# Per-head norms of the first attention layer: one power on GpSimd for a bit-pattern guess with Newton steps

## The chip, the cores and the metric

The kernel runs on one core of a Trainium2 chip. The metric is the device time of one execution in microseconds (us). The kernel before took 2115.83 us in the median of 3 runs, from 2112.31 to 2118.05. The trace comes from one further, profiled execution.

## The reference, cut to what matters

The input is 16 batches of 512 tokens with 128 features. Two transformer layers run over it, each with an attention and a mixture of experts, each behind a layer norm and with a residual. The change concerns the attention of the first layer. It has 16 heads of 8 features; q and k are scaled to length one for each head, and no softmax is taken:

```
def _l2norm(t):
    n = jnp.sqrt(jnp.sum(t * t, axis=-1, keepdims=True))
    return t / jnp.maximum(n, 1e-12)
q = _l2norm(proj(Wq, bq)); k = _l2norm(proj(Wk, bk)); v = proj(Wv, bv)
sim = jnp.einsum('bhid,bhjd->bhij', q, k)
out = jnp.einsum('bhij,bhjd->bhid', sim / n ** sigmoid(m), v)
```

The kernel forms k^T v before it multiplies by q, so only the two scalings stand between the projection and the next products: for each token 32 numbers, 1/sqrt(max(sum of squares, 1e-24)), one for each head of q and of k.

## The kernel before, in words

A batch of 512 tokens is held as 128 partitions by Q = 4 rows of 128 features. Batches run through a software pipeline: `looped` (L276 is its loop) alternates an `x_phase` and a `y_phase`, and in one turn four batches are worked on at once under the names f (front: first attention and first experts), r (the second layer's projections), b (the second layer's scores, softmax and outputs) and t (tail: output projection, residual, router). Three turns are written out ahead of the loop, 13 run in it, and some phases follow it. After the loop comes the second layer's expert routing and the experts, which the change doesn't touch.

Each engine has its own program and its order is written by hand; engines wait for each other by semaphores alone. In the `y_phase` the vector engine (DVE) runs, in this order: `r_norm`, `f_bias`, `r_center`, `f_bias`, `f_l2`, `r_rest` 0, `f_scale`, `r_rest` 1, `outputs` 0 (the copy of the product in `bo` to `oT`, L1379), `norm` 0 (L1386, L1388), `f_kvm`, and so on to the gates of the first experts and `norm` 3, with which the turn of the loop ends.

- `f_l2` waits for the squares `sq` that the scalar engine (ACT, L1026) makes of q and k, sums them by head (L1180), takes the maximum with 1e-24 (L1181), makes a first guess of 1/sqrt by integer arithmetic on the bits (L1182) and does one Newton step (L1187 to L1189). `f_scale` does two more and multiplies k and q by the result `rn` (L1196). All of these but L1196 are done in two halves of two rows each: while a half waits for its own result, the other runs. Each half is followed by a wait of DVE on its own semaphore.
- `r_rest` (L1372) subtracts the rounded part of the second layer's q or k from the product in `facc`. GpSimd (POOL) then rounds the rest and subtracts again (L485, L487). SP writes the three parts of both to memory (`part_dmas`) and, when both are written, reads them back spread over partitions as QT and KT (`back_dmas`, L329).
- `power` (L451) is POOL's 1/sqrt: a TENSOR_TENSOR with the operation pow and a tile of -0.5, `mhalf`, 128 columns wide. It is used for the layer norms' four numbers a partition.
- PE (TensorE), in the same phase, runs the second layer's scores of a pair of heads (`pair_scores`, 10 products with their masks, L579 and L581), and between them `outputs` (L838), `turn_outputs` (L845, which waits for DVE's `oT`) and the front batch's products: `f_kvq` (L620), `f_kv` (L627, L630), which waits for L1196, `f_kvo`, `f_out`. Scores go through three banks of PSUM, which ACT's exponentials (L1017) empty.

Of the kernel before, what the change touches and what calls it, by code (L numbers as in the profile page):

```python
# [14 lines left out]
F32, BF16, F16, I32, I16 = mybir.dt.float32, mybir.dt.bfloat16, mybir.dt.float16, mybir.dt.int32, mybir.dt.int16  # L15
ALU = mybir.AluOpType
# [3 lines left out]
P = 128  # L20
BATCH, SEQ, D = 16, 512, 128
Q = SEQ // P
TOK = BATCH * SEQ
TILES = TOK // P
HEADS, HD = 16, 8
# [7 lines left out]
L2_EPS_SQ = 1e-24  # L33
# [11 lines left out]
def build_kernel(nc, a, out):  # L45
    ctx = ExitStack()
    with ctx:
# [5 lines left out]
        def sb1(name, shape, dt=F32):  # L53

            return early.enter_context(nc.sbuf_tensor(name, shape, dt))

        def sem(name):
            return ctx.enter_context(nc.semaphore(name))
# [55 lines left out]
        f_rs = sb1("f_rs", [P, Q])  # L114
        n2 = sb1("n2", [P, Q, 2 * HEADS])
        rn = sb1("rn", [P, Q, 2 * HEADS])
        rt = sb1("rt", [P, Q, 2 * HEADS])
        f_n = sb1("f_n", [P, Q, D])
        f_nT = sb1("f_nT", [P, SEQ])
        kvq = sb1("kvq", [P, Q, 3 * D])  # L120
# [64 lines left out]
        def sb3(name, shape, dt=F32):  # L185
# [51 lines left out]
        contrib = [sb(f"contrib{i}", [P, CC, D]) for i in range(2)]  # L237


        names = """s_wfront s_wexperts s_wback s_cst s_one s_scal s_x s_lnf s_xres s_varf s_rsf s_T1 s_nT1 s_kvq s_kvqe s_sq  # L240
            s_kqn s_kvt s_kvm s_qT s_qnT s_kvo s_kvoc s_at0 s_x1 s_x1n s_T2 s_nT2 s_lgm s_lge s_exf s_lgx s_gp s_gTp s_gT
            s_h1 s_h3 s_gb s_gbc s_sil s_t s_h s_hs s_ym s_yT s_yTt s_x2 s_fc
            s_pad s_lnb s_varb s_rsb s_T3 s_nT3 s_q s_k s_v s_p1 s_r1 s_p2 s_p3 s_vp s_qkw s_qk0 s_qk1 s_S s_red s_nmp s_nmt
# [4 lines left out]
        S = {n: sem(n) for n in names}  # L248
# [3 lines left out]
        def apart(eng):  # L252

            eng.nop(nofuse=True)
# [165 lines left out]
        def _(pool):  # L420
# [28 lines left out]
            def power(dst, src, ready, done, count):  # L449
                pool.wait_ge(S[ready], count)  # L450
                pool.tensor_tensor(dst, src, mhalf[:, 0:src.shape[-1]], ALU.pow).then_inc(S[done], 1)  # L451
# [25 lines left out]
            def y_phase(b, f, r, t):  # L477
                if r is not None:
                    power(b_rs[:], b_ve[:], "s_varb", "s_rsb", r + 1)
                if r is not None:  # L480
                    for w in range(2):

                        pool.wait_ge(S["s_r1"], 2 * r + w + 1)
                        apart(pool)
                        pool.tensor_copy(qkp[:, w, 1], qkr[:, w]).then_inc(S["s_p2"], 1)  # L485
                        pool.wait_ge(S["s_p2"], 2 * r + w + 1)
                        pool.tensor_tensor(qkp[:, w, 2], qkr[:, w], qkp[:, w, 1], ALU.subtract).then_inc(S["s_p3"], 1)  # L487
                if f is not None:
                    power(f_rs[:, 0:Q], f_ve[:, 0:Q], "s_varf", "s_rsf", 2 * f + 2)

            looped(pool, x_phase, y_phase)
            for m in range(1 - GJ, GJ):

# [598 lines left out]
        def _(dve):  # L1092
# [35 lines left out]
                    dve.wait_ge(self.sem, self.b * self.per + self.n)  # L1128
                    apart(dve)

            fc, mc, rc, tc = Steps("s_fc", 67), Steps("s_mstep", 6), Steps("s_rstep", 8), Steps("s_tc", 8)

            def stats(step, x, st, mv):

# [41 lines left out]
            def f_l2(f):  # L1176


                dve.wait_ge(S["s_sq"], f + 1)
                fc.halves(lambda q: dve.tensor_reduce(n2[:, q], sq[:, q].rearrange("p q (g d) -> p (q g) d", d=HD), X, ALU.add))  # L1180
                fc.halves(lambda q: dve.tensor_scalar(n2[:, q], n2[:, q], L2_EPS_SQ, None, ALU.max))  # L1181
                fc.halves(lambda q: dve.tensor_scalar(rn[:, q].bitcast(I32), n2[:, q].bitcast(I32), -0.5, float(0x5F3759DF), ALU.mult, ALU.add))  # L1182
                f_newton(1)

            def f_newton(steps):
                for _ in range(steps):
                    fc.halves(lambda q: dve.scalar_tensor_tensor(rt[:, q], n2[:, q], -0.5, rn[:, q], ALU.mult, ALU.mult))  # L1187
                    fc.halves(lambda q: dve.tensor_tensor(rt[:, q], rt[:, q], rn[:, q], ALU.mult))
                    fc.halves(lambda q: dve.scalar_tensor_tensor(rn[:, q], rt[:, q], 1.5, rn[:, q], ALU.add, ALU.mult))  # L1189

            def f_scale(f):
                f_newton(2)
                fc.join()
                for w in range(2):
                    heads = kvq[:, :, 2 * w * D:(2 * w + 1) * D].rearrange("p q (h d) -> p q h d", d=HD)
                    last = dve.tensor_tensor(heads, heads, rn[:, :, w * HEADS:(w + 1) * HEADS, None].to_broadcast([P, Q, HEADS, HD]), ALU.mult)  # L1196
                last.then_inc(S["s_kqn"], 1)
# [176 lines left out]
            def y_phase(b, f, r, t):  # L1374
# [26 lines left out]
                if_r(r_center)  # L1401
                if_f(lambda f: f_bias(f, 1))
                if_f(f_l2)
                if_r(r_rest, 0)
                if_f(f_scale)
                if_r(r_rest, 1)
                outputs(0)
# [227 lines left out]
```

## Time and profile before

| | before |
|---|---|
| median of 3 runs | 2115.83 us |
| the profiled execution | 2124.21 us |
| its span, first to last instruction | 2122.4 us |
| granted TensorE clock, mean | 0.881 of full |
| busy: PE, DVE, ACT, POOL | 1623.8, 1243.4, 793.3, 502.1 us |
| one turn of the loop, about | 106 us |

Busy time is the sum of the instructions of an engine; waits and register instructions aren't in it. The chain of waits starts at the last instruction and goes back from each step to what released it, so what stands on it sets the time. "issue" in a view is time in which an engine waited for nothing that the profile shows.

### The profile page before, as it was taken

How to read it: one execution, taken by the hardware profiler on the slowest of the kernel's cores; microseconds unless marked ns; L12 is line 12 of the kernel's file. 1: busy time of each engine (PE TensorE's matmuls, PEld its weight loads, DVE VectorE, ACT ScalarE, POOL GpSimd, SP SyncE). 2: the span in 40 equal slices, each digit the busy share in tenths (PEclk: the TensorE clock that was granted, in tenths of full speed). 3: DMA queues.
4: the chain of work that ended last, by engine and by line, in shares of the span. 5: the costliest groups of instructions: out<-in, count | busy, mean ns of one | idle time of the engine just before them, and what ended most of it. 6: DMA issues, size and time to landing. Idle time of an engine off the chain costs nothing.

```text
span 2122.4 us, 34602 instructions
## 1 busy us (share of the span) xinstructions
PE 1623.8 (77%) x10136; PEld 908.2 (43%) x10136; DVE 1243.4 (59%) x3733; ACT 793.3 (37%) x1515; POOL 502.1 (24%) x487
## 2 busy tenths in 40 slices
PE   3779888888888888888888888888899781137675
PEld 2345444444444444444444444444454441135554
DVE  5466757575757575757575757575766436861111
ACT  1225252525252525252525252525253342233331
POOL 2321212121212121212121212121212002007887
PEclk7879999989898989899999898999999875568888
DMA  2032231313131313131313031313031400023443
GB/s 64 19 46 41 31 53 24 52 24 58 18 56 20 58 18 58 18 54 22 56 19 59 17 59 17 56 20 59 17 56 21 65 7 10 0 35 84 90 92 59
DMA packets 113451, 86.62 MB, mean 41 GB/s; under 512 B 21440, under 2 KB 107840, under 8 KB 113344
## 3 DMA queue, kind: packets, MB, share of 16 engines
q1 hardware_dynamic: 102080, 76.64, 21.7%
q0 software_dynamic: 11264, 8.92, 3.0%
q14 instruction: 85, 0.70, 0.2%
q8 instruction: 22, 0.36, 0.1%
HBM read 59.02 MB, written 25.72 MB: 40 GB/s over the span
## 4 chain that ended last, share of the span: by engine, by line
PE 44%; issue 18%; DVE 17%; ACT 5%; POOL 5%; DMA 5%; SPq 2%; DVEq 1%; ACTq 0%; POOLq 0%
PE ba L579 6%; PE fa L668 5%; PE facc L694 5%; PE ba L584 4%; PE fa L684 4%; PE bo L838 4%; POOL out L551 3%; ACT probs L1017 2%; SPq L329 2%; DVE passed L1464 2%; PE ba L581 2%; PE ba L586 2%; DVE nm L1264 2%; DMA KT<-qk_parts 1%; POOL got L521 1%
## 5 line engine op out<-in xcount | busy, mean ns | idle before, releaser
L584 PE MATMUL ba<-KT,QT 72*128 72x512 bf16 (+3 forms) x1024 | 263.9, 321 | 188.5 <-DVE nm L1264 130.5
L1017 ACT ACTIVATE probs<-ba 128x512 f32<-128x512 f32 x640 | 330.3, 634 | 94.9 <-PE ba L581 94.0
L458 POOL TENSOR_TENSOR hh<-th,gb 128x512 f32<-128x512 f32 x128 | 162.1, 1267 | 713.5 <-ACT gb L970 437.2
L1264 DVE TENSOR_REDUCE nm<-ba 128x1 f32<-128x512 f32 x256 | 174.8, 683 | 191.7 <-issue 142.6
L579 PE MATMUL ba<-QT,KT 75*128 75x512 bf16 (+3 forms) x1024 | 254.8, 311 | 35.3 <-ACT probs L1017 28.9
L584 PEld LDWEIGHTS ba<-KT,QT 72*128 72x128 bf16 x1024 | 105.2, 103 | 350.2 <-DVE nm L1264 155.2
L586 PE MATMUL ba<-mask_q,identb 128*128 128x128 bf16 x1024 | 201.7, 231 | 0.0
L581 PE MATMUL ba<-mask_k,identb 128*128 128x128 bf16 x1024 | 197.1, 225 | 0.0
L668 PE MATMUL fa<-f_nT,w 128*128 128x512 f32 x320 | 187.1, 669 | 2.3 <-ACT sc L1048 1.2
L684 PE MATMUL fa<-f_nT,w 128*128 128x512 f32 x320 | 181.0, 649 | 0.0
L986 ACT ACTIVATE sil<-fa 128x512 f32<-128x512 f32 x160 | 95.1, 594 | 213.8 <-PE fa L668 213.6
L970 ACT ACTIVATE gb<-fa 128x512 f32<-128x512 f32 x128 | 76.3, 596 | 260.8 <-PE fa L676 260.7
L579 PEld LDWEIGHTS ba<-QT,KT 75*128 75x128 bf16 x1024 | 102.4, 100 | 155.2 <-ACT probs L1017 100.8
L694 PE MATMUL facc<-hh,w 128*128 128x512 f32 x320 | 166.2, 602 | 0.0
L838 PE MATMUL bo<-probs,vp 128*32 128x512 f32 (+3 forms) x2048 | 155.6, 445 | 0.8 <-DVE ao L1388 0.8
L1266 DVE TENSOR_REDUCE nm<-ba 128x1 f32<-128x384 f32 x256 | 140.6, 549 | 24.5 <-PE ba L586 24.4
L586 PEld LDWEIGHTS ba<-mask_q,identb 128*128 128x128 bf16 x1024 | 106.5, 104 | 82.6 <-issue 80.3
L451 POOL TENSOR_TENSOR b_rs<-b_ve,mhalf 128x4 f32<-128x4 f32 x48 | 48.5, 1010 | 338.8 <-DVE b_ve L1364 228.1
L1379 DVE COPY oT<-bo 128x512 f32<-128x512 f32 x64 | 44.1, 689 | 116.7 <-PE bo L838 116.7
L551 POOL DMA_INDIRECT out<-contrib,cur x64 | 100.7, 1573 | 29.4 <-issue 18.6
L838 PEld LDWEIGHTS bo<-probs,vp 128*32 128x32 f32 x2048 | 60.9, 112 | 101.6 <-issue 76.2
L581 PEld LDWEIGHTS ba<-mask_k,identb 128*128 128x128 bf16 x1024 | 103.3, 101 | 1.8 <-issue 0.9
(283 smaller groups left out, 2681.2 us busy)
## 6 DMA issues: line engine op xcount, KB each, us to landing
QT<-qk_parts SPq DMA_DIRECT2D x288, 64.0 KB
KT<-qk_parts SPq DMA_DIRECT2D x288, 64.0 KB
qk_parts<-qkp SPq DMA_DIRECT2D x32, 384.0 KB, 2.5
fc<-in_L_ffn_fc_weight SPq DMA_DIRECT2D x32, 256.0 KB, 2.9
xin<-in_L_attn_x SPq DMA_DIRECT2D x16, 256.0 KB, 14.3
out<-x SPq DMA_DIRECT2D x16, 256.0 KB, 2.3
xn_rows<-row SPq DMA_DIRECT2D x16, 256.0 KB, 2.4
w<-in_L_w SPq DMA_DIRECT2D x3, 640.0 KB, 6.9
```

What stands on the lines that cost most here:

```text
L458: pool.tensor_tensor(hh[:, e % 2], th[:, e % 2], gb[:, e % 2], ALU.mult).then_inc(S["s_h"], 1)
L551: pool.indirect_dma_start(out_rows, bass.IndirectOffsetOnAxis(cur[k][:, c:c + 1], 0), contrib[k % 2][:, c], None, compute_op=ALU.add).then ...
L579: pe.matmul(bank[:, col:col + w], lhsT=KT[0:K_ROWS, head, blk * P:(blk + 1) * P], rhs=QT[0:K_ROWS, head, blk * P:], start=True, stop=False)
L581: last = pe.matmul(bank[:, col:col + P], lhsT=identb[:], rhs=mask_k[:], start=False, stop=True)
L584: pe.matmul(bank[:, col:col + w], lhsT=QT[0:QK_ROWS, head, blk * P:(blk + 1) * P], rhs=KT[0:QK_ROWS, head, 0:w], start=True, stop=False)
L586: last = pe.matmul(bank[:, col + w - P:col + w], lhsT=identb[:], rhs=mask_q[:], start=False, stop=True)
L668: pe.matmul(fa[0][:], lhsT=w1[:, e], rhs=f_nT[:], start=True, stop=True).then_inc(S["s_h1"], 1)
L684: pe.matmul(fa[1][:], lhsT=w3[:, e], rhs=f_nT[:], start=True, stop=True).then_inc(S["s_h3"], 1)
L694: pe.matmul(facc[:], lhsT=w2[:, e], rhs=hh[:, e % 2], start=e == 0, stop=e == U0 - 1).then_inc(S["s_ym"], 1)
L838: last = pe.matmul(bo[32 * j:32 * j + 32, blk * P:], lhsT=vp[:, blk, 4 * k + j], rhs=prob_block(4 * k + j, blk), start=blk == 0, stop=blk ...
L1017: act.activation(probs[:, pair % 3, f_], ba[n % 3][:], ACT.Exp, scale=SCALE).then_inc(S["s_exp"], 1)
L1264: last = dve.tensor_reduce(nm[:, 3, h:h + 1], bank[:], X, ALU.max, negate=True)
```

## The change

The guess, the three Newton steps and the tile `rt` go. DVE takes the maximum in one instruction over all 128 numbers and signals `s_n2`; POOL raises them to -0.5 in one instruction and signals `s_rn`; `f_scale` on DVE waits for that. On POOL the power stands in the `y_phase` behind the power of the second layer's norm and ahead of the two casts and subtractions of the rests. On DVE `r_rest` 0 stays between `f_l2` and `f_scale`.

```
@@ y_phase of POOL @@
                 if r is not None:
                     power(b_rs[:], b_ve[:], "s_varb", "s_rsb", r + 1)
+                if f is not None:
+                    power(rn[:].rearrange("p q g -> p (q g)"), n2[:].rearrange("p q g -> p (q g)"), "s_n2", "s_rn", f + 1)
                 if r is not None:
                     for w in range(2):
@@ DVE @@
-            fc, mc, rc, tc = Steps("s_fc", 67), Steps("s_mstep", 6), Steps("s_rstep", 8), Steps("s_tc", 8)
+            fc, mc, rc, tc = Steps("s_fc", 45), Steps("s_mstep", 6), Steps("s_rstep", 8), Steps("s_tc", 8)
...
                 fc.halves(lambda q: dve.tensor_reduce(n2[:, q], sq[:, q].rearrange("p q (g d) -> p q g d", d=HD), X, ALU.add))
-                fc.halves(lambda q: dve.tensor_scalar(n2[:, q], n2[:, q], L2_EPS_SQ, None, ALU.max))
-                fc.halves(lambda q: dve.tensor_scalar(rn[:, q].bitcast(I32), n2[:, q].bitcast(I32), -0.5, float(0x5F3759DF), ALU.mult, ALU.add))
-                f_newton(1)
-
-            def f_newton(steps):
-                for _ in range(steps):
-                    fc.halves(lambda q: dve.scalar_tensor_tensor(rt[:, q], n2[:, q], -0.5, rn[:, q], ALU.mult, ALU.mult))
-                    fc.halves(lambda q: dve.tensor_tensor(rt[:, q], rt[:, q], rn[:, q], ALU.mult))
-                    fc.halves(lambda q: dve.scalar_tensor_tensor(rn[:, q], rt[:, q], 1.5, rn[:, q], ALU.add, ALU.mult))
-
+                fc.join()
+                dve.tensor_scalar(n2[:], n2[:], L2_EPS_SQ, None, ALU.max).then_inc(S["s_n2"], 1)
             def f_scale(f):
-                f_newton(2)
-                fc.join()
+                dve.wait_ge(S["s_rn"], f + 1)
                 for w in range(2):
```

## Rows read from the trace of the kernel before

**Rows 1.** The page: the span and each engine's busy time, share and instructions.

```profile
span 2122.4 us, 34602 instructions
PE 1623.8 (77%) x10136; PEld 908.2 (43%) x10136; DVE 1243.4 (59%) x3733; ACT 793.3 (37%) x1515; POOL 502.1 (24%) x487
```

**Rows 2.** The chain of waits, 1015 to 1058 us: start us, us, what.

```profile
1017.82 1.11 ACT sq L1026
...
1023.75 0.82 issue
...
1026.58 0.69 DVE kvq L1196
1027.26 0.60 DVE qkr L1372
1027.86 0.61 DVE oT L1379
1028.52 0.66 PE bo L845 x4
```

**Rows 3.** Timeline of DVE: start us, us, line, tile; idle before and releaser.

```profile
1014.11 0.17 DVE L1364 TENSOR_SCALAR b_ve<-b_mv 128x4 f32<-128x4 f32 x1 [0.47 <-DVE b_mv L1138]
...
1015.40 1.12 DVE L1143 TENSOR_SCALAR b_n<-x,b_mv,b_rs 128x128 f32 x4
...
1018.95 1.28 DVE L1180 TENSOR_REDUCE n<-sq 128x64 f32<-128x512 f32 x2 [1.50 <-ACT sq L1026]
...
1021.90 0.68 DVE L1372 TENSOR_TENSOR qkr<-facc,qkp 128x512 f32<-128x512 f32 x1
1022.50 0.35 DVE L1187 SCALAR_TENSOR_TENSOR rt<-n,rn 128x64 f32<-128x64 f32 x2
1022.82 0.72 DVE L1188 TENSOR_TENSOR rt<-rt,rn 128x64 f32<-128x64 f32 x2
1023.51 1.27 DVE L1189 SCALAR_TENSOR_TENSOR rn<-rt,rn 128x64 f32<-128x64 f32 x2
...
1025.11 0.40 DVE L1188 TENSOR_TENSOR rt<-rt,rn 128x64 f32<-128x64 f32 x2
1025.46 0.40 DVE L1189 SCALAR_TENSOR_TENSOR rn<-rt,rn 128x64 f32<-128x64 f32 x2
1025.97 1.29 DVE L1196 TENSOR_TENSOR kvq<-kvq,rn 128x512 f32<-128x512 f32 x2
...
1027.78 0.68 DVE L1379 COPY oT<-bo 128x512 f32<-128x512 f32 x1
...
1030.84 0.29 DVE L1201 TENSOR_TENSOR kvm<-fa,kv_scale 128x128 f32<-128x128 f32 x1 [1.04 <-PE fa L627]
```

**Rows 4.** Timeline of PE in the same turn.

```profile
1024.24 2.36 PE L838 MATMUL bo<-probs,vp 128*32 128x512 f32 x32
```

**Rows 5.** Waits (us in total, times, longest), and DVE's and PE's timeline at the jump.

```profile
DVE nm L1264 <- issue: 142.6, 12, 12.9
1068.25 0.69 DVE L1264 TENSOR_REDUCE nm<-ba 128x1 f32<-128x512 f32 x1 [12.40 <-issue]
1069.00 0.50 PE L584 MATMUL ba<-KT,QT 72*128 72x384 bf16 x1 [11.40 <-DVE nm L1264]
```

**Rows 6.** Timeline of POOL in the turn of rows 3.

```profile
1014.36 1.01 POOL L451 TENSOR_TENSOR b_rs<-b_ve,mhalf 128x4 f32<-128x4 f32 x1 [14.77 <-DVE b_ve L1364]
1022.72 0.61 POOL L485 CAST qkp<-qkr 128x512 bf16<-128x512 f32 x1 [7.35 <-DVE qkr L1372]
1023.41 1.16 POOL L487 TENSOR_TENSOR qkp<-qkr,qkp 128x512 bf16<-128x512 f32 x1
```

**Rows 7.** Timeline of DVE in the first batch.

```profile
26.94 1.28 DVE L1180 TENSOR_REDUCE n<-sq 128x64 f32<-128x512 f32 x2 [1.12 <-ACT sq L1026]
...
32.22 1.29 DVE L1196 TENSOR_TENSOR kvq<-kvq,rn 128x512 f32<-128x512 f32 x2
```

**Rows 8.** Groups of POOL by line and shape: count, busy us, mean ns, idle before.

```profile
L458 POOL TENSOR_TENSOR hh<-th,gb 128x512 f32<-128x512 f32 x128 | 162.1, 1267 | 713.5 <-ACT gb L970 437.2 <-DVE th L1253 269.9 <-PE facc L694 6.4
L451 POOL TENSOR_TENSOR b_rs<-b_ve,mhalf 128x4 f32<-128x4 f32 x48 | 48.5, 1010 | 338.8 <-DVE b_ve L1364 228.1 <-DVE b_ve L1286 100.4 <-DVE b_ve L1296 10.3
L451 POOL TENSOR_TENSOR f_rs<-f_ve,mhalf 128x4 f32<-128x4 f32 x32 | 32.3, 1010 | 203.3 <-DVE f_ve L1210 191.5 <-DVE f_ve L1165 11.7
L516 POOL TENSOR_TENSOR ahead<-weight 128x8 f32<-128x8 f32 x1 | 0.2, 205 | 0.0
```

**Rows 9.** Stretches: busy us (count) by engine, granted clock, DMA share, GB/s.

```profile
1065.00:1069.00 4.00, 0.00 (x1) 0.01 (x1) 0.75 (x2) 0.00 (x0) 0.00 (x0) 0.50 0.59 67
1069.00:1071.00 2.00, 2.00 (x6) 1.04 (x7) 2.00 (x5) 0.00 (x0) 0.00 (x0) 0.50 0.59 66
1071.00:1073.00 2.00, 2.00 (x9) 0.90 (x7) 0.72 (x3) 0.90 (x2) 0.08 (x1) 0.52 0.29 58
1073.00:1075.00 2.00, 2.00 (x12) 1.10 (x11) 1.38 (x3) 0.78 (x2) 1.18 (x1) 1.00 0.00 0
```

**Rows 10.** DMA queues, 1055 to 1069 us: packets, MB, share of 16 engines.

```profile
q1 hardware_dynamic: 1247, 1.03, 61.7%
q14 instruction: 2, 0.02, 0.9%
```

**Rows 11.** One turn as a stretch, columns as in rows 9.

```profile
1008.00:1113.00 105.00, 86.67 (x569) 46.17 (x568) 68.01 (x209) 42.70 (x84) 19.89 (x18) 0.95 0.26 38
```

More of the change, by code:

```diff
@@ L116, in build_kernel @@
         rn = sb1("rn", [P, Q, 2 * HEADS])
-        rt = sb1("rt", [P, Q, 2 * HEADS])
         f_n = sb1("f_n", [P, Q, D])
@@ L237, in build_kernel @@
         contrib = [sb(f"contrib{i}", [P, CC, D]) for i in range(2)]
-        names = """s_wfront s_wexperts s_wback s_cst s_one s_scal s_x s_lnf s_xres s_varf s_rsf s_T1 s_nT1 s_kvq s_kvqe s_sq
+        names = """s_wfront s_wexperts s_wback s_cst s_one s_scal s_x s_lnf s_xres s_varf s_rsf s_T1 s_nT1 s_kvq s_kvqe s_sq s_n2 s_rn
             s_kqn s_kvt s_kvm s_qT s_qnT s_kvo s_kvoc s_at0 s_x1 s_x1n s_T2 s_nT2 s_lgm s_lge s_exf s_lgx s_gp s_gTp s_gT
```

## The prediction

> **What bounds the kernel now.** I read the page first. No engine fills the span: PE is busy 77% of it, DVE 59%, POOL 24% [rows 1]. So the question is which chain sets the pace of a batch, and what the share of an engine is worth has to be read in the stage that changes. The chain of waits came next. In the stage that holds the change (1017 to 1030 us, one of the steady turns of the loop) it runs ACT `sq`, then DVE through the Newton steps to `kvq` L1196, `qkr` L1372 and the copy `oT` L1379, and only then PE's transposes L845 [rows 2]. The reader is to see that DVE, not PE, is on the path there: PE had finished the product that `oT` copies at 1024.24 + 2.36 = 1026.60, and `oT` started at 1027.78 [rows 3, 4]. Everything in `f_scale` therefore stands in front of the batch, and an engine that makes `f_scale` late makes the batch late by as much. The same turn ends with 12.4 us in which DVE and PE stand still after the jump back of the loop [rows 5]; I come to it below.
>
> **What is removed.** 22 DVE instructions a batch (11 steps in two halves): the two maxima, the two guesses, 18 halves of Newton steps. In time that is the stretch from the end of the sum of squares, 1018.95 + 1.28 = 1020.23, to the start of L1196 at 1025.97: 5.74 us [rows 3]. It is not all arithmetic: 0.60 us of it is the rest L1372 (1021.90 to 1022.50), which stays, and about 1.2 us is lost while POOL casts and subtracts (1022.72 to 1024.57) [rows 6]: the two halves of L1188 took 0.72 instead of 0.40 and those of L1189 1.27 instead of 0.40 [rows 3]. For the very first batch, with no other work beside it, the stretch is 26.94 + 1.28 = 28.22 to 32.22, so 4.0 us [rows 7].
>
> **What is added.** One maximum over 128x128 on DVE, at most the 0.29 us of L1201, another one of that size [rows 3]; a semaphore from DVE to POOL (0.08 us: L1364 ends at 1014.28, L451 starts at 1014.36) and one back (0.03 us: L451 ends at 1015.37, L1143 starts at 1015.40) [rows 3, 6]; and one power of 128 columns on POOL, of length P.
>
> P is not in the trace: all 80 powers there have 4 columns and take 1.01 us [rows 8]. Bounds from the nearest rows: an ordinary two-input POOL instruction takes 0.205 us for 8 columns and 1.267 us for 512 [rows 8], 2.1 ns a column. If the power's excess of 1.010 - 0.205 = 0.805 us is paid once an instruction, P = 1.01 + 124 x 0.0021 = 1.3 us. If it is paid by the column, that is 0.201 us a column, and P = 1.01 + 124 x 0.201 = 25.9 us. If all of the 1.01 us scales, P = 32 x 1.01 = 32.3 us. I take 25.9: L516 does everything that an instruction of this shape needs once, for twice the columns, in 0.205 us, so the excess belongs to evaluating the function, and that is done for each column; a once-only cost would be four times that whole instruction.
>
> A rule of the Trainium skill speaks for the short end. The GPSIMD Engine Reference (section 3.1) gives about 2.6 cycles an element for a two-input elementwise instruction at 1.2 GHz; an estimate from it is 0.27 us for 124 more columns and P = 1.28 us. The slope between L516 and L458 agrees with it, but the L451 rows do not fit it at all, since by it a power of 4 columns would cost about what L516 costs. By it the sum would be that of the first rival.
>
> **The sum.** With P = 25.9 the power ends at 1020.23 + 0.3 + 0.08 + 25.9 = 1046.5 and `f_scale` starts at 1046.6 instead of 1025.97: 20.6 us late. For the first batch it is 0.3 + 0.1 + 25.9 - 4.0 = 22.3. Nothing covers it. Queued on DVE behind the wait are L1196, the second rest, the copies of PE's output and all later steps of the phase; the first rest stands ahead of the wait and runs under the power. On POOL, behind the power, stand the cast and subtraction of the first rest; they would have run at 1022.72 and now start at 1046.5. They gate the write of the parts and so SP's loads of QT and KT, but SP waits for the second rest's parts too before it loads, and those come after L1196 in any case, so the loads shift with the batch and not beyond it. PE can still do the first output product and three scores of the next pair, as it does now, and then waits for `oT`.
>
> Two smaller terms. The cast and subtraction now meet L1196, which reads two SBUF tensors as L1188 and L1189 do: I add the 1.2 us they lost, for 15 batches, 18 us. And PE stands still for about 20 us in each phase. After the 11.4 us of idling at the loop's end the granted clock is 0.50 (1.2 GHz) in the rows, and it stays there for about 4 us of work before 1.00 (2.4 GHz) is back [rows 9]; 4 us at half speed cost 2 us, in the 14 phases that have scores: 28 us.
>
> Sum: 15 x 20.6 + 22.3 = 331, + 18 + 28 = **+377 us**. The profiled execution took 2124.2 us (span 2122.4), 0.4% above the median of the three runs, 2115.8, and its stages are taken as those of a median run: 2116 + 377 = **2493 us**.
>
> **The loop's jump.** DVE starts its first instruction of the next turn 12.4 us after the last one of this turn, 12 of these waits sum to 142.6 us and nothing in the program releases them [rows 5]. In that stretch queue 14, which carries instructions, moves 2 packets, while the loads of QT and KT fill the queues [rows 10]. The change takes 22 of DVE's 209 instructions of a turn [rows 11], and their waits, out of the loop. I price that at nothing: the jump is still there and still falls into the loads of QT and KT. The bounds are both sides of nothing: -143 us if the shorter body no longer has to be brought in again, and up to +60 (12 turns x 5 us, a little under half of a present wait) if the packets come at a worse moment.
>
> The Trainium skill (Runtime: NRT & Kernel Launch, section Instruction fetch mechanics) says that a taken branch whose target is no longer in the engine's instruction window stalls on a DMA fetch. The two packets in the stretch agree; whether the shorter loop would fit no run here shows.
>
> **Rivals.**
> 1. *The power's excess is paid once* (P = 1.3). It is the other side: `f_scale` is then ready at 1022.5, behind the first rest, meets POOL's cast and subtraction (+1.2), and `oT` starts when PE is done, at 1026.6 instead of 1027.78. 14 x 1.2 + 2 x 2.3 (first two batches: 4.0 - 1.7) = 21 us less: 2095 us. It decides from P = 1025.97 - 1020.23 - 0.3 - 0.1 = 5.3 us, 35 ns a column: below it the change gains, above it loses. For it: POOL's ordinary slope is 2.1 ns. Against: the 0.8 us that no other small POOL instruction has.
> 2. *Columns overlap inside the instruction*, so that further ones cost half of what the first four did: P = 13.5, 8.2 us a batch, 16 x 8.2 + 18 + 28 = +177: 2293 us. No row tells it from the forecast.
> 3. *The loop body, shorter, stays in place*, with the slow power: 2493 - 143 = 2350 us. For it: 22 of 209 instructions of a turn go [rows 11]. Against it: a tenth is little, and the trace shows no loop of DVE that is as long and does not wait.
>
> **How the numbers follow.** Forecast 0.70, rival 1 0.10, rival 2 0.13, rival 3 0.07. The forecast's own range goes from 2440 (without the clock and contention terms) to 2640 (P = 32.3 adds 16 x 6.4 = 102, the fetches up to 60; both in full are unlikely). The full range reaches down over rivals 3 and 2: **2200 to 2640**; what it leaves out is rival 1 and the tails, under 2 in 10. A difference under 0.3% (about 6 us) can't be told from none in this kernel. Faster: rival 1 less its part near the break-even, 0.09; within 0.3%: 0.02; slower: 0.89.
>
> **What would show it.** In the profile after: a POOL group `rn<-n,mhalf` 128x128 x16 near 26 us (right), near 1.3 or 13 us (rivals 1, 2); DVE idle before the scaling of `kvq` (L1196 now), released by POOL, some 24 us each, 16 times; DVE's busy time down by the Newton steps, worth nothing; a granted clock of 0.50 around the restart in mid-phase; the issue wait of the loop's jump still near 12 us (rival 3: gone). The prediction is wrong if the power is under 10 us, or if the batch grows by clearly less or more than the power outlasts the Newton steps.

## The result, and the profile after

| | before | after |
|---|---|---|
| median in the same runs | 2116.94 us (2112.31 to 2118.59, 4 runs) | 2429.31 us (2422.09 to 2435.56, 4 runs) |
| ratio over the runs, 95% interval | 1 | 1.1491, 1.1449 to 1.1533 |
| the profiled execution | 2124.21 us, span 2122.4 | 2434.28 us, span 2432.5 |
| granted TensorE clock, mean | 0.881 | 0.833 |

The change costs 312 us where +377 were forecast. First the page of the changed kernel, the lines that answer to [rows 1] and the shares of its chain of waits:

```profile
span 2432.5 us, 33657 instructions
PE 1660.3 (68%) x10136; PEld 937.9 (39%) x10136; DVE 1189.3 (49%) x3397; ACT 795.2 (33%) x1515; POOL 838.9 (34%) x503
PE 35%; issue 23%; POOL 19%; DVE 12%; DMA 3%; SPq 2%; ACT 2%; DVEq 1%; POOLq 0%; ACTq 0%
```

DVE's busy time fell by 54.1 us (1243.4 to 1189.3), and that bought nothing. POOL's rose by 337, and POOL, 5% of the chain before, is now 19% of it. Three groups of after and, as the last line, the scaling of before say where (busy us, mean ns of one, then the idle time ahead and its releaser):

```profile
L450 POOL TENSOR_TENSOR rn<-n,mhalf 128x128 f32<-128x128 f32 x16 | 332.5, 20781 | 94.5 <-DVE n L1183 94.5
L450 POOL TENSOR_TENSOR b_rs<-b_ve,mhalf 128x4 f32<-128x4 f32 x48 | 48.5, 1011 | 335.0 <-DVE b_ve L1356 223.0 <-DVE b_ve L1278 102.0 <-DVE b_ve L1288 10.0
L1188 DVE TENSOR_TENSOR kvq<-kvq,rn 128x512 f32<-128x512 f32 x32 | 40.8, 1314 | 305.4 <-POOL rn L450 305.4
L1196 DVE TENSOR_TENSOR kvq<-kvq,rn 128x512 f32<-128x512 f32 x32 | 20.7, 689 | 1.7
```

The new power takes 20.78 us each time, and DVE stands 305 us in front of the scaling of `kvq`, released by it. The scaling itself takes 1314 ns instead of 689: it now starts together with POOL's cast (1104.22 and 1104.14 below). Now one turn in time order, DVE, POOL and PE one after the other (start, duration, instruction, in brackets the idle time ahead and what ended it):

```profile
1081.72 1.28 DVE L1181 TENSOR_REDUCE n<-sq 128x64 f32<-128x512 f32 x2 [1.73 <-ACT sq L1027]
1083.10 0.23 DVE L1183 TENSOR_SCALAR n<-n 128x128 f32<-128x128 f32 x1
1084.66 0.69 DVE L1364 TENSOR_TENSOR qkr<-facc,qkp 128x512 f32<-128x512 f32 x1 [1.33 <-ACT qkp L971]
1104.22 2.63 DVE L1188 TENSOR_TENSOR kvq<-kvq,rn 128x512 f32<-128x512 f32 x2 [18.87 <-POOL rn L450]
1106.78 0.68 DVE L1364 TENSOR_TENSOR qkr<-facc,qkp 128x512 f32<-128x512 f32 x1
1107.38 0.67 DVE L1371 COPY oT<-bo 128x512 f32<-128x512 f32 x1
```

```profile
1083.41 20.78 POOL L450 TENSOR_TENSOR rn<-n,mhalf 128x128 f32<-128x128 f32 x1 [5.63 <-DVE n L1183]
1104.14 0.61 POOL L486 CAST qkp<-qkr 128x512 bf16<-128x512 f32 x1
1104.83 1.47 POOL L488 TENSOR_TENSOR qkp<-qkr,qkp 128x512 bf16<-128x512 f32 x1
```

```profile
1087.02 2.36 PE L839 MATMUL bo<-probs,vp 128*32 128x512 f32 x32
1108.11 1.12 PE L846 MATMUL bo<-ident,oT 128*128 128x128 f32 x4 [17.74 <-DVE oT L1371]
```

The chain is the one forecast: power, scaling, second rest, copy, transposes. PE finished the product that L1371 copies at 1087.02 + 2.36 = 1089.38, went on with scores until 1090.37 and was idle from there to 1108.11. From the windows of the same turn (length, then busy time of PE, PEld, DVE, ACT and POOL with counts, granted clock, DMA share, GB/s), the clock of that pause, which answers to [rows 9]:

```profile
1092.00:1094.00 2.00, 0.00 (x0) 0.00 (x0) 0.00 (x0) 0.00 (x0) 2.00 (x1) 1.00 0.00 0
1096.00:1098.00 2.00, 0.00 (x0) 0.00 (x0) 0.00 (x0) 0.00 (x0) 2.00 (x1) 0.50 0.00 0
1110.00:1112.00 2.00, 2.00 (x12) 1.94 (x11) 0.00 (x0) 1.10 (x2) 0.00 (x0) 0.50 0.57 197
1112.00:1114.00 2.00, 1.99 (x17) 1.43 (x17) 0.29 (x1) 1.30 (x3) 0.00 (x0) 1.00 0.15 42
```

PE works again from 1108.11 and gets 0.50 until 1112. The loop's jump waits as before [rows 5]; the first line is of the waits (total, times, longest), the second of DMA in the stretch 1137 to 1150:

```profile
DVE nm L1256 <- issue: 143.8, 12, 13.4
q14 instruction: 2, 0.02, 0.8%
```

To see where 310 us of span went, I cut each turn at DVE's own instructions (the jump runs from the branch to the first register instruction behind it) and took the mean over the turns with a jump ahead of them (12 of 13), in us:

| stage of a turn | before | after | e4_busy | e5_pages | e8_castfirst |
|---|---|---|---|---|---|
| wait at the jump | 11.97 | 12.08 | 12.45 | 0.29 | 11.92 |
| x_phase, to the residual sum L1355 | 49.50 | 49.81 | 49.60 | 51.27 | 49.86 |
| to the sum of squares L1180 | 7.45 | 7.45 | 7.45 | 7.45 | 7.45 |
| sum of squares to scaling L1196 | 7.02 | 22.50 | 22.50 | 22.51 | 26.39 |
| scaling to first `oT` L1379 | 1.98 | 3.16 | 3.16 | 3.16 | 1.81 |
| to second `oT` | 8.00 | 9.98 | 7.98 | 10.17 | 10.25 |
| to third `oT` | 7.87 | 7.87 | 7.87 | 7.87 | 7.87 |
| to fourth `oT` | 8.15 | 9.24 | 8.27 | 8.41 | 9.48 |
| to the branch | 3.85 | 4.16 | 4.16 | 3.81 | 4.16 |
| one turn | 105.80 | 126.25 | 123.46 | 114.93 | 129.19 |

After against before: +20.45 in each of 12 turns (245.5), +16.4 in the loop's first turn, +50.6 in the three batches ahead of it, -2.4 behind the loop: 310.1, the difference of the spans.

### The profile page after: what moved, and what is told of

Same layout as the page of the kernel before. It is cut to its first block, busy times and chain, and to the rows that moved or that the text cites. A ratio compares the mean times of both kernels' runs of the same rounds, so it can differ in the third digit from the quotient of the medians.

```text
span 2432.5 us, 33657 instructions
## 1 busy us (share of the span) xinstructions
PE 1660.3 (68%) x10136; PEld 937.9 (39%) x10136; DVE 1189.3 (49%) x3397; ACT 795.2 (33%) x1515; POOL 838.9 (34%) x503
## 4 chain that ended last, share of the span: by engine, by line
PE 35%; issue 23%; POOL 19%; DVE 12%; DMA 3%; SPq 2%; ACT 2%; DVEq 1%; POOLq 0%; ACTq 0%
POOL rn L450 13%; PE ba L580 5%; PE bo L839 5%; PE fa L669 4%; PE fa L685 3%; PE ba L585 3%; POOL out L552 3%; PE facc L695 3%; PE ba L582 2%; DVE passed L1456 2%; SPq L328 2%; POOL got L522 1%; PE ba L587 1%; PE bo L846 1%; DMA xin<-in_L_attn_x 1%
## 5 line engine op out<-in xcount | busy, mean ns | idle before, releaser
L450 POOL TENSOR_TENSOR rn<-n,mhalf 128x128 f32<-128x128 f32 x16 | 332.5, 20781 | 94.5 <-DVE n L1183 94.5
L580 PE MATMUL ba<-QT,KT 75*128 75x512 bf16 (+3 forms) x1024 | 264.9, 320 | 35.2 <-ACT probs L1018 28.7
L1256 DVE TENSOR_REDUCE nm<-ba 128x1 f32<-128x512 f32 x256 | 174.4, 681 | 191.4 <-issue 143.8
L846 PE MATMUL bo<-ident,oT 128*128 128x128 f32 x256 | 46.8, 313 | 252.6 <-DVE oT L1371 252.6
L582 PE MATMUL ba<-mask_k,identb 128*128 128x128 bf16 x1024 | 204.0, 231 | 0.0
L1188 DVE TENSOR_TENSOR kvq<-kvq,rn 128x512 f32<-128x512 f32 x32 | 40.8, 1314 | 305.4 <-POOL rn L450 305.4
L839 PE MATMUL bo<-probs,vp 128*32 128x512 f32 (+3 forms) x2048 | 163.8, 464 | 0.8 <-DVE ao L1380 0.8
L846 PEld LDWEIGHTS bo<-ident,oT 128*128 128x128 f32 x256 | 31.0, 157 | 264.6 <-DVE oT L1371 262.7
```

Source lines behind the costliest of these rows:

```text
L580: pe.matmul(bank[:, col:col + w], lhsT=KT[0:K_ROWS, head, blk * P:(blk + 1) * P], rhs=QT[0:K_ROWS, head, blk * P:], start=True, stop=False)
L582: last = pe.matmul(bank[:, col:col + P], lhsT=identb[:], rhs=mask_k[:], start=False, stop=True)
L839: last = pe.matmul(bo[32 * j:32 * j + 32, blk * P:], lhsT=vp[:, blk, 4 * k + j], rhs=prob_block(4 * k + j, blk), start=blk == 0, stop=blk ...
L1256: last = dve.tensor_reduce(nm[:, 3, h:h + 1], bank[:], X, ALU.max, negate=True)
```

## The experiments

Ratios are against the kernel before, run on the same chip, and taken over the runs, so they aren't the quotients of the medians (2120.57 us for e2 to e5, 2124.45 for e1 and e6 to e8, 2123.09 for e9 and e10). Theory A is the prediction's account of each step unless the expectation says otherwise.

**e1_widths: what a power costs by width.** The kernel before, with instructions like these ahead of everything:

```
+for n in (1, 2, 4, 8, 16, 32, 64, 128):
+    pool.tensor_tensor(res[:, 0:n], base_c[:, 0:n], mhalf[:, 0:n], ALU.pow)
+pool.tensor_tensor(res[:], base_v[:], mhalf[:], ALU.pow)      # 128 different bases
+pool.tensor_tensor(res[:], base_c[:], two[:], ALU.pow)        # exponent 2
...
```

> The kernel before, with twelve more POOL instructions ahead of everything else, each waited for: the power -0.5 of 0.7 over 1, 2, 4, 8, 16, 32, 64 and 128 columns, the power -0.5 of varied numbers over 128 columns, the power 2 of 0.7 over 128 columns, and a multiplication over 4 and 128 columns. Theory A, a fixed part and 0.16 us a column: 0.5, 0.6, 1.0, 1.6, 2.9, 5.4, 10.5 and 20.8 us; the same 20.8 whatever the numbers and the exponent; the multiplications 0.20 and 0.45. Theory B, the time depends on the numbers: the varied ones and the exponent 2 differ from the constant ones by more than a tenth. Its time as a kernel is of no interest (some 45 us more at the start).

POOL's groups by shape, of the line with the constant base (L452), the different bases (L453), exponent 2 (L454) and a multiply of 128 columns (L456):

```profile
L452 POOL TENSOR_TENSOR res<-base_c,mhalf 128x1 f32<-128x1 f32 x1 | 0.6, 612 | 0.1
L452 POOL TENSOR_TENSOR res<-base_c,mhalf 128x4 f32<-128x4 f32 x1 | 1.0, 1010 | 0.1
L452 POOL TENSOR_TENSOR res<-base_c,mhalf 128x16 f32<-128x16 f32 x1 | 2.9, 2898 | 0.1
L452 POOL TENSOR_TENSOR res<-base_c,mhalf 128x64 f32<-128x64 f32 x1 | 10.5, 10547 | 0.1
L452 POOL TENSOR_TENSOR res<-base_c,mhalf 128x128 f32<-128x128 f32 x1 | 20.8, 20780 | 0.1
L453 POOL TENSOR_TENSOR res<-base_v,mhalf 128x128 f32<-128x128 f32 x1 | 20.8, 20770 | 0.1
L454 POOL TENSOR_TENSOR res<-base_c,two 128x128 f32<-128x128 f32 x1 | 20.8, 20770 | 0.1
L456 POOL TENSOR_TENSOR res<-base_v,mhalf 128x128 f32<-128x128 f32 x1 | 0.5, 453 | 0.1
```

The cost is a straight line: (20.780 - 10.547) / 64 = 0.160 us a column, and 1.010 - 4 x 0.160 = 0.37 us once. The line holds from 2 columns on; one column takes 0.61 us instead of 0.53. The 128 different bases and the exponent 2 cost the same as the constant base and -0.5. The multiply of the same 128 columns takes 0.45 us. The one time of the whole kernel, 2204.75 us, holds 12 such instructions at its start (86 us by their rows, where the expectation said 45) and says nothing more.

**e2_mult: the same wait, a cheap operation.** The changed kernel, with

```
-power(rn[:].rearrange("p q g -> p (q g)"), n2[:].rearrange("p q g -> p (q g)"), "s_n2", "s_rn", f + 1)
+pool.wait_ge(S["s_n2"], f + 1)
+pool.tensor_tensor(rn[:].rearrange("p q g -> p (q g)"), n2[:].rearrange("p q g -> p (q g)"), mhalf[:], ALU.mult).then_inc(S["s_rn"], 1)
```

> The changed kernel with a multiplication by -0.5 in the power's place, same tiles, same order, same waits (it leaves out the 1/sqrt of the norms). Theory A, the length of the power is the whole loss: POOL's instruction takes some 0.5 us instead of 20.78, the scaling of kvq starts right behind the first rest, and the time is that of rival 1 of the prediction, 2095 us, 1% under the kernel before; no wait of DVE for POOL there, the granted clock back where it was. Theory B, moving the step to POOL costs as such (two semaphores more, the casts queued behind it, the reading of SBUF by two engines at once): 2117 us or more.

2105.47 us (2094.57 to 2107.25), ratio 0.992 (0.989 to 0.9949). In the waits the scaling's idle time, 305.4 us of after, shrinks to

```profile
DVE kvq L1189 <- POOL rn L481: 0.6, 1, 0.6
DVE nm L1257 <- issue: 148.1, 12, 13.4
```

So the move to POOL with its two semaphores costs nothing; the whole loss is the power's duration. The gain is 15 us, not the first rival's 21: `oT` does start earlier, but a turn is only 0.30 us shorter than before (105.50), with 0.46 us more at the jump (12.43) and 0.31 more in the stage ahead of the branch. Over 12 turns that is 4 us. Of the 17.8 us between the two spans (2122.4 and 2104.6) 9.9 lie in the three batches ahead of the loop, and 5.2 behind the loop, where no such step runs; why that part is shorter stays open.

**e3_half: the power on 64 of the 128 columns,** the other 64 multiplied:

```
+pool.tensor_tensor(rn[:, 2:]..., n2[:, 2:]..., mhalf[:, 0:64], ALU.mult).then_inc(S["s_rn"], 1)
+pool.tensor_tensor(rn[:, 0:2]..., n2[:, 0:2]..., mhalf[:, 0:64], ALU.pow).then_inc(S["s_rn"], 1)
```

> The changed kernel with the power on 64 of the 128 columns, the other 64 multiplied by -0.5 (it leaves out the 1/sqrt of half the norms). Theory A, a fixed part of 0.37 us and 0.159 us a column (from 1.01 us for 4 columns and 20.78 for 128): the power takes 10.6 us, with the multiplication in front 10.9, each batch is 9.9 us shorter than with 128 columns, 16 x 9.9 = 158: 2271 us. Theory B, the cost depends on the call and not on the columns beyond some width: the power stays near 20 us and the time near 2430. Theory C, the clock's share shrinks with the wait (PE idles 10 us less in mid-phase): up to 28 us less than A, 2243.

2270.82 us (2263.23 to 2274.74), ratio 1.0711 (1.0666 to 1.0756). POOL's group, and DVE's wait:

```profile
L482 POOL TENSOR_TENSOR rn<-n,mhalf 128x64 f32<-128x64 f32 x16 | 168.8, 10548 | 0.0
DVE kvq L1190 <- POOL rn L482: 146.2, 16, 11.0
```

The power is 10.2 us shorter, and with the multiplication ahead of it the scaling starts 9.95 us earlier (12.55 us behind the sum of squares, 22.50 in after). 16 times that is 159 us, and the kernel is 158 us faster than after: each us of P goes into the time. Theory C isn't borne out: the stage from the first to the second `oT` still takes 9.92 us.

**e4_busy: is the stage behind the pause slow because of the clock?** Products without a reader fill PE's pause ahead of the transposes:

```
+def keep_busy(f):
+    pe.wait_ge(S["s_kvqe"], Q * f + Q)
+    for _ in range(19):
+        pe.matmul(fa[1][:], lhsT=w_kvq[:, 0:D], rhs=f_nT[:], start=True, stop=True)
-pair_scores(3, lambda: turn_outputs(0))
+pair_scores(3, lambda: (if_f(keep_busy), turn_outputs(0)))
```

> The changed kernel with 19 products of 128x128 by 128x512 (f32) on PE, into a free bank, right where PE waits for the copy oT; their results are never read. Theory A, PE's idling costs clock: the granted clock stays at 1.00 through the wait, the stage between the first and second copy oT goes back from 9.98 to 8.00 us in 14 batches (28 us), and the second dip that four batches show in a later stage (3.3 us each, 13 us) goes too: 2429 - 28 to 41 = 2388 to 2401. Theory B, the two microseconds come from something else (the loads of QT and KT, the order of the exponentials): 2429 us or, with more products in PE's queue, above it.

2401.87 us (2396.49 to 2409.13), 27 us less than after and just short of the 28 to 41 expected, ratio 1.1348 (1.1299 to 1.1397); mean clock 0.889 instead of 0.833. The stage from the first to the second `oT` is back at 7.98 us (table above), and the four transposes take what they took at full clock:

```profile
1094.23 0.66 PE L851 MATMUL bo<-ident,oT 128*128 128x128 f32 x4 [1.38 <-DVE oT L1376]
```

0.66 us instead of 1.12. In the windows from 1076 to 1098 of this trace the granted clock is 1.00 throughout. The 2 us a turn were the clock, granted at 0.50 because PE had stood still.

**e5_pages: the place of the loop in DVE's program.** In the loops of before and after, DVE pauses for some 0.4 us at each 128th instruction (waits and register instructions counted), and queue 14, which carries instructions, moves packets of 8 KB, five in each turn. I call 128 instructions a page. One such pause in after, behind the 353rd instruction of the loop:

```profile
1135.90 0.17 DVE L1233 CAST gparts<-gates 128x16 bf16<-128x16 f32 x1 [0.35 <-DVE gparts L1233]
```

The loop of before has 438 instructions and that of after 373, not 22 fewer: the waits of the removed steps count. After's loop begins 31 instructions behind a page's start (31 + 353 = 384, three pages, is where the pause above stands): 31 + 373 = 404 lies in four pages. That of before begins 32 behind one: 470, four as well. The edit moves after's loop to 4 behind a start, so that 377 lie in three (the 102 steps are 101 instructions more in DVE's trace):

```
+for _ in range(102):
+    dve.wait_ge(S["s_scal"], 5)
+    apart(dve)
```

> The changed kernel with 101 instructions more ahead of DVE's loop, waits on a semaphore that is long there; the loop itself is unchanged at 373 instructions. In the trace DVE hesitates 0.4 us every 128 instructions and a packet of 8 KB (128 instructions) is read there, and the loop of the changed kernel begins 31 instructions behind such a place, so it touches four such pages, the last with 20 instructions; with the 101 it begins 4 behind one and touches three. Theory A, a loop whose pages and the one read ahead are four or fewer stays in the engine: the waits of 143.8 us at the jump go, and with them the slow clock behind them (12 x 2 us): 2429 - 140 to 165 = 2264 to 2289. Theory B, every jump back reads its target anew however the code lies: 2429 us, issue wait 143 us as before.

2312.55 us (2300.33 to 2325.5), ratio 1.0926 (1.0859 to 1.0992): 117 us faster than after, with 101 instructions more. Queue 14 and the jump, first after, then e5_pages:

```profile
q14 instruction: 84, 0.69, 0.1%
DVE nm L1256 <- issue: 143.8, 12, 13.4
```

```profile
q14 instruction: 25, 0.20, 0.0%
DVE nm L1259 <- issue: 0.6, 3, 0.2
DVE f_st L1137 <- DMA xin<-in_L_attn_x: 45.9, 14, 6.3
```

59 packets and the whole wait are gone. The Trainium skill (Runtime: NRT & Kernel Launch, section Instruction fetch mechanics) gives fetch blocks of 16 KiB and a window of two of them, so 512 instructions. The measurement differs, and decides: the packets here are of 8 KB, 377 instructions from a page's start in three pages stay (375 in e6_whole), and 404 in four are fetched again (416 in e7_whole4, 470 in before). Blocks of 256 don't give it from either start. The loops of after, e6_whole and e7_whole4 begin in one page of the program, those of before and e5_pages in the next; if the next one opens a block, before's 470 would stay, and if it closes one, after's 404 and e7_whole4's 416 would. The gain of e5_pages is below the 140 to 165 us expected: the start takes 12.9 us longer, the x_phase 1.5 us a turn, and the third line names a new wait, for the front batch's input, 45.9 us in 14 turns and hardly there in the kernel before (two waits, 5.6 us) and in after (two, 4.9 us).

**e6_whole: Newton kept, loop in three pages.** The kernel before, with every step in halves done whole. This leaves 365 instructions, beginning 10 behind a page's start:

```
 def halves(self, op):
-    for half in range(2):
-        ...
+    self(op(slice(0, Q)))
```

> The kernel before, Newton steps and all, with every step of the first layer's norms and gates done over the whole tile and waited for, and not in two halves: DVE's loop falls from 438 to 365 instructions and, where it now lies, begins 10 behind the start of a stretch of 128 and touches three of them. Theory A: a step over the whole takes about as long as two halves one behind the other (0.36 us), and the wait of 12 us at the loop's jump goes, as it went with the 101 instructions ahead of the changed kernel's loop (117 us there): 2119 - 117 to 140 = 1979 to 2002 us. Theory B: whole steps lay each instruction's own latency bare, 0.1 to 0.2 us in 24 steps of 16 batches: 40 to 80 us of it are lost again, 2020 to 2080 us.

2046.31 us (2036.92 to 2052.2), ratio 0.9623 (0.9577 to 0.9669). That is theory B's range, but not for its reason: e7_whole4, below, prices the whole steps at some 11 us. The 12 us at the jump no longer stand in the waits. Its next limit does:

```profile
q14 instruction: 24, 0.20, 0.0%
DVE f_st L1128 <- DMA xin<-in_L_attn_x: 74.6, 14, 7.2
```

**e7_whole4: the control.** e6_whole with 41 instructions ahead of the loop, which now begins 51 behind a page's start: 51 + 365 = 416, four pages.

```
+for _ in range(42):
+    dve.wait_ge(S["s_scal"], 5)
+    apart(dve)
```

> The kernel of whole steps with 41 instructions more ahead of DVE's loop, waits on a semaphore that is long there: the same 365 instructions begin 51 behind the start of a stretch of 128 and touch four. Theory A: the wait at the jump is there again, 12 us in 12 turns, and the time is that of the kernel before, 2119 us, more or less by what whole steps cost. Theory B, the gain of the kernel without them is due to fewer instructions: the same time as there.

2135.21 us (2124.34 to 2142.76), ratio 1.0056 (1.0026 to 1.0085). The jump's wait and the packets are back, the wait for the input is not:

```profile
q14 instruction: 84, 0.69, 0.1%
DVE nm L1259 <- issue: 142.3, 12, 13.3
DVE f_st L1128 <- DMA xin<-in_L_attn_x: 7.3, 2, 4.8
```

The same instructions in the loop, 89 us apart by where it begins. It also shows what the halves are worth: without them, in four pages, the kernel is 0.56% slower (11 us) than before.

**e8_castfirst: is the slow scaling contention?** The changed kernel with the power behind the cast and subtraction of the first rest, so that neither runs beside the scaling:

```
+if f is not None and w == 0:
+    power(rn[:]..., n2[:]..., "s_n2", "s_rn", f + 1)
```

> The changed kernel with the power of 128 columns behind POOL's cast and subtraction of the first rest instead of ahead of them. The power starts 3.8 us later (1024.5 instead of 1020.7 on the clock of the trace before). Theory A, the cast and subtraction are what makes the two scalings of kvq take 2.6 us instead of 1.3: the stage from the scaling to the first copy oT goes back from 3.16 to 1.98 us, the net is 2.6 us in 15 batches: 2429 + 39 = 2468. Theory B, the scalings are slow for another reason (they follow the power): 3.8 us in 15 batches, 2486.

2476.66 us (2468.79 to 2483.25), ratio 1.1655 (1.1603 to 1.1707). The total lies between the two numbers and doesn't decide; the row does:

```profile
L1190 DVE TENSOR_TENSOR kvq<-kvq,rn 128x512 f32<-128x512 f32 x32 | 20.7, 688 | 362.2 <-POOL rn L450 362.2
```

The scaling takes 688 ns again, and the stage behind it fell from 3.16 to 1.81 us. The power comes 3.89 us later for it, so the order of the change is the better one. The stage after it stayed slow (10.25 us), as it should if the clock does that, since PE stands still here too.

**e9_xearly and e10_xonly: where the rest of e6's gain went.** SP asks for the input `xin` after QT's and KT's loads, at the top of the next turn. The edit moves the request between the two halves of these loads (and writes the last turn out), in e9 on e6_whole, in e10 on the kernel before:

```
 part_dmas(i + 1)
-both(back_dmas, i + 1)
+back_dmas(i + 1, 0)
+load_x(i + 3)
+back_dmas(i + 1, 1)
```

> The kernel of e6_whole, and SP asks for the next-but-two batch's input `xin` between the two halves of the loads of QT and KT instead of behind both. Nothing is left out. In e6_whole DVE waits 74.6 us in 14 turns for `xin`, in the kernel before 5.6. Theory A (with the jump wait gone, the input that SP asks for last is what is late next, and this is where the rest of the expected gain went): that wait falls below 15 us and the time from 2046 to 1975 to 2005 us. Theory B (the DMA queues are the limit: whatever is asked for earlier pushes the second half of QT and KT back by the 17 us that `xin` takes): 2035 to 2070 us, with PE's wait for KT grown by as much as DVE's for `xin` falls.

> The kernel before with the same edit of SP's order alone, as a control. Nothing is left out. Theory A: DVE hardly waits for `xin` there (5.6 us in all), since every turn stands still 12 us at the jump anyway; no change within 0.5%, and the issue wait at the jump between 120 and 150 us in all. Theory B (an earlier `xin` pushes back KT): 10 to 60 us slower.

e9: **1964.76 us** (1954.65 to 1973.98), ratio 0.9272 (0.924 to 0.9305). DVE's wait for the input falls from 74.6 us to a single one of 3.9, and a turn takes 92.67 us instead of e6's 99.69. PE's waits for KT are 23.8 us, 20.6 in e6; the weight loads (PEld) wait in the same stretches, so their 18.6 is not added:

```profile
DVE f_st L1137 <- DMA xin<-in_L_attn_x: 3.9, 1, 3.9
PE ba L593 <- DMA KT<-qk_parts: 23.8, 10, 10.1
PEld ba L593 <- DMA KT<-qk_parts: 18.6, 4, 10.4
```

That is theory A, and 10 us beyond its range. e10: 2111.99 us (2096.27 to 2115.35), ratio 0.9937 (0.9912 to 0.9963): a small gain, just beyond the 0.5% expected; its jump waits 129.4 us where before waits 142.6. The early request is worth 3.5% (0.9623 to 0.9272, some 75 us) once the jump is gone, and 0.6% beside it.

## Why the prediction was right, and where it was off

**The bound: right.** DVE's chain through `f_scale` into `oT` was on the path, and what it lost came out in the time: e2_mult and e3_half move P alone and the time follows it.

**P: the term that was mis-sized.** The step "1.01 + 124 x 0.201 = 25.9" charged the whole 0.805 us above an ordinary instruction to the four columns. The mechanism, by the column, was right; 0.37 us of the 1.01 are paid once, not 0.205, and a column costs 0.160 us. P is 20.78 us, within the bounds given (1.3 to 32.3). With it the prediction's own sum is 1020.23 + 0.38 + 20.78 - 25.97 = 15.4 us late instead of 20.6 (measured: 22.50 - 7.02 = 15.48), and for the first batch 0.4 + 20.78 - 4.0 = 17.2 instead of 22.3 (measured from the start of the sum of squares to that of the scaling: 22.51 - 5.28 = 17.23). That is 15 x 15.4 + 17.2 = 248 instead of 331, and with the other two terms +294, where +312 was measured.

**Contention: right.** +1.2 a turn forecast, 3.16 - 1.98 = 1.18 measured; e8_castfirst takes the neighbour away and the scaling is back at 688 ns.

**Clock: right, and short of one piece.** +2 a turn forecast, 9.98 - 8.00 = 1.98 measured; e4_busy takes the idling away and the stage is at 7.98. Not foreseen: in 4 of the 12 turns the clock falls a second time, later in the phase, and the stage to the fourth `oT` takes 11.43 us instead of 8.14. In such a turn:

```profile
1252.00:1254.00 2.00, 0.82 (x8) 0.39 (x6) 0.00 (x0) 1.60 (x4) 0.00 (x0) 1.00 0.57 61
1258.00:1260.00 2.00, 2.00 (x12) 0.47 (x16) 1.30 (x7) 0.00 (x0) 0.00 (x0) 0.50 0.58 61
```

PE is at work in the second window, and had been idle for 1.18 us around 1253. Over 12 turns this is 13 us. It isn't tied to the long pause: e6_whole, which has no power of 128 columns and no such pause, shows it in 6 of its 12 turns (9.76 us each, granted clock 0.83 on the mean of the stage) and e10_xonly in 3, while before and e3_half show it in none; and the idle piece of 1.18 us stands in the turns without it too. So the mean of 8.27 in e4_busy (one turn of 12 is slow) doesn't show that filling the long pause removes it, and why it strikes these turns stays open. Of the rest, the 0.31 us ahead of the branch is the pause at a page's edge shown under e5_pages: where that edit moves the edge elsewhere, the stage is back at 3.81. The 0.31 us in the x_phase and 0.11 at the jump, 5 us in all, no run here settles.

**The jump: priced right, by luck.** 143.8 us after, 142.6 before. But "a tenth is little" wasn't the reason. The loop lost 65 instructions, not 22, and by the count of pages it would have stayed in place if it had begun up to 384 - 373 = 11 instructions behind a page's start. It began 31 behind. Rival 3, at 0.07, was a matter of where the code fell: with 101 instructions ahead it came true, at -117 instead of -143.

**The rivals.** Rival 1 (paid once) fell with P. Its break-even of 5.3 us lies between the two runs nearest to it, and no run is closer: at 0.45 us e2_mult is faster than before, at 10.55 us e3_half is slower. Rival 2 (further columns at half price) predicted 13.5 us; columns after the fourth cost the same as each other, and the price is four fifths of what the first four suggested.

## What to carry to other kernels

Before an elementwise function is moved to another engine, get its price at two widths: a row at one small width can't part what is paid once from what is paid by the column, and the product with 16 batches decides the sign. Ask what the step it replaces had cost on the path (5.74 us here), not how many instructions go. And count a hot loop's instructions on its engine, waits included, against the pages in which they are fetched: here three pages instead of four were worth 89 to 117 us, and what that uncovered (an input asked for too late) another 75.

## What the runs showed of the hardware that was not expected

- POOL's power costs 0.160 us a column and 0.37 us once, from 2 columns (0.70 us) to 128 (20.78 us), and the same for the bases and the two exponents tried; a multiply of 128 columns takes 0.45 us.
- DVE's program is read in packets of 8 KB, 128 instructions. Loops of 365 and 373 instructions that lay in three of them were not read again (24 or 25 packets in the whole run), and at a jump DVE waited 0.29 us; in four of them they were read each turn (84 packets) and the jump took about 12 us beside the loads of QT and KT.
- In some turns (4 of 12 in after, 6 of 12 in e6_whole) the granted clock falls to 0.50 while PE is at work; its longest pause in the 12 us before is 1.18 us, and the turns without a fall have the same pause.
